# Expert rows transposed by their load, and one 32 by 32 product per head in the mamba stage

## The reference

```python
x = x + 0.5 * ffn(layernorm(x))      # mixture of experts
x = x + mamba(layernorm(x))
x = x + 0.5 * ffn(layernorm(x))      # the same weights again
```

## Time and profile before

| | us |
|---|---|
| median of 3 runs (1732.28 to 1732.94) | 1732.43 |
| the profiled execution | 1741.65 |
| its span | 1739.9 |
| TensorE busy | 1276.7 (73%) |
| VectorE busy | 1325.7 (76%) |
| ScalarE busy | 724.0 (42%) |
| GpSimd busy | 654.1 (38%) |
| DMA | 104.66 MB, mean 60 GB/s |

### The profile page before, as it was taken

The page is one execution under the profiler, slowest core; times in us unless marked ns, Lnnn a source line. Parts: engine busy times, 40 slices in busy tenths (PEclk is TensorE's granted clock), DMA queues, the critical chain, the costliest instruction groups (busy, mean ns, idle before and its releaser), DMA issues.

```text
span 1739.9 us, 32954 instructions
## 1 busy us (share of the span) xinstructions
PE 1276.7 (73%) x10560; PEld 961.0 (55%) x10560; DVE 1325.7 (76%) x3687; ACT 724.0 (42%) x1586; POOL 654.1 (38%) x832
## 2 busy tenths in 40 slices
PE   3426999947887787777888777688876551799990
PEld 3416999933545455454545445454544441799990
DVE  5964777758988888888888888898885664577776
ACT  2323555514444444444444444444444220355550
POOL 3873333323434343333424343333422376233330
PEclk9999999968878888888878788888878555899995
DMA  8543333310000000000000000000000022333328
GB/s 216 183 168 88 95 97 94 84 34 13 16 22 13 25 14 18 20 16 21 15 24 14 24 13 18 20 16 22 16 16 11 33 86 89 89 94 93 94 81 302
DMA packets 86838, 104.66 MB, mean 60 GB/s; under 512 B 18192, under 2 KB 66320, under 8 KB 86672
## 3 DMA queue, kind: packets, MB, share of 16 engines
q1 hardware_dynamic: 67856, 59.31, 13.2%
q0 software_dynamic: 14208, 39.05, 6.1%
q10 hardware_dynamic: 4608, 4.20, 0.7%
HBM read 50.88 MB, written 43.23 MB: 54 GB/s over the span
## 4 chain that ended last, share of the span: by engine, by line
PE 35%; DVE 22%; SPq 13%; POOL 9%; DMA 8%; issue 8%; ACT 5%; another core or an unknown queue 0%; POOLq 0%; DVEq 0%; ACTq 0%
SPq L1068 11%; PE bank L641 11%; PE bank L655 11%; DMA yg<-ychosen 5%; POOL disp L545 4%; ACT y L1115 4%; PE bank L1175 4%; DVE cv L876 3%; DVE cv L879 3%; PE bank L1242 2%; POOL arena L1028 2%; PE bank L1225 2%; DVE X L816 2%; PE bank L624 2%; DMA y<-y 1%
## 5 line engine op out<-in xcount | busy, mean ns | idle before, releaser
L590 POOL DMA_INDIRECT ychosen<-arena,didx x144 | 139.8, 971 | 295.1 <-ACT arena L687 280.1
L641 PE MATMUL bank<-arena,weights 128*128 128x128 f16 x3456 | 221.0, 221 | 0.0
L655 PE MATMUL bank<-weights,arena 128*128 x1728 | 211.5, 273 | 0.0
L641 PEld LDWEIGHTS bank<-arena,weights 128*128 x3456 | 203.3, 99 | 0.6 <-issue 0.3
L676 ACT ACTIVATE arena<-bank 128x512 f32<-128x512 f32 x144 | 86.0, 597 | 240.9 <-issue 140.3
L717 DVE TENSOR_TENSOR arena<-arena 128x512 f32<-128x512 f32 x144 | 99.8, 693 | 105.8 <-ACT arena L676 104.4
L1206 PE MATMUL bank<-arena,cst 128*128 128x512 f32 x256 | 172.4, 810 | 0.0
L655 PEld LDWEIGHTS bank<-weights,arena 128*128 128x128 f16 x1728 | 163.2, 98 | 16.4
L545 POOL DMA_INDIRECT disp<-arena,sloti x128 | 132.6, 1036 | 65.2 <-issue 39.8
L876 DVE TENSOR_SCALAR cv<-U,vec 128x128 f32<-128x128 f32 x160 | 141.7, 948 | 0.0
L1014 POOL TENSOR_TENSOR Hs<-Hs,dd 64x512 f32<-64x512 f32 x32 | 34.3, 1071 | 282.4 <-DVE yi L916 268.3
(11 more groups left out here) (168 smaller groups left out, 2646.7 us busy)
## 6 DMA issues: line engine op xcount, KB each, us to landing
arena<-disp SPq DMA_DIRECT2D x144, 129.5 KB
arena<-in_w SPq DMA_DIRECT2D x16, 512.0 KB
yg<-ychosen SPq DMA_DIRECT2D x32, 256.0 KB, 2.8
y<-y SPq DMA_DIRECT2D x512, 16.0 KB, 1.8
arena<-ychosen SPq DMA_DIRECT2D x32, 256.0 KB, 5.9
X<-in_x SPq DMA_DIRECT2D x32, 128.0 KB, 4.6
out<-X ACTq DMA_DIRECT2D x32, 128.0 KB, 6.1
ychosen<-arena,didx POOLq DMA_INDIRECT x144
```

Source lines behind the costliest of these rows:

```text
L590: pool.indirect_dma_start(ychosen, bass.IndirectOffsetOnAxis(ap=didx[:, t % NIDX:t % NIDX + 1], axis=0), ysb[t % YB][:, :], None).then_inc ...
L641: mm = pe.matmul(o, chunk(where, 2 * ("hl".index(w) * WN + c * HID + m * P), P), v, start=c == 0 and n_ == 0, stop=c == KD - 1 and n_ == 2)
L655: mm = pe.matmul(o, x, chunk(where, 2 * ((2 + "hl".index(w)) * WN + c * D), D), start=c == 0 and n_ == 0, stop=c == KH - 1 and n_ == 2)
```

## The change

The expert load becomes two: one that transposes the 512 halves into `xTh` (now eight buffers), and a small one for the last 6 halves of each row into `xtail`. TensorE's `turn` and VectorE's copy are gone; SP waits for `up` in place of `turned`. In mamba each pair's 64x64 product becomes two products, each with 32 weight columns and 32 moving columns, all into bank 6; ScalarE copies a half at once, and the two waits that bank 7 needed are gone.

```diff
-XIN, YB, HB = 4, 3, 3
+XIN, YB, HB = 8, 3, 3
...
-        xin = [carve(ROW, F16) for p in range(XIN)]
-        xTh = [carve(4 * P, F16) for p in range(2)]
+        xTh = [carve(4 * P, F16) for p in range(XIN)]
+        xtail = [carve(ROW - 2 * D, F16) for p in range(XIN)]
...
                 if t >= XIN:
-                    sp.wait_ge(S("turned"), n - XIN + 1)
+                    sp.wait_ge(S("up"), n - XIN + 1)
                     sp.wait_ge(S("didx"), n - XIN + 1)
-                sp.dma_start(xin[t % XIN][:, :], disp[ds(at, P), :]).then_inc(S(f"xin_{t % XIN}"), 16)
+                sp.dma_start(xTh[t % XIN].rearrange("p (c t) -> p c t", t=P), disp[ds(at, P), 0:2 * D], transpose=True)\
+                    .then_inc(S(f"xin_{t % XIN}"), 16)
+                sp.dma_start(xtail[t % XIN], disp[ds(at, P), 2 * D:ROW]).then_inc(S(f"xtail_{t % XIN}"), 16)
...
-            def turn(t):
+            def up(t):
                 n = r * NS + t
                 pe.wait_ge(S(f"xin_{t % XIN}"), 16 * (t // XIN + 1 + r * (NS // XIN)))
                 if n >= 2:
-                    pe.wait_ge(S("xth"), n - 1)
-                for c in range(4):
-                    m = pe.transpose(banks[t % 2].bitcast(F16)[:, c * P:(c + 1) * P], xin[t % XIN][:, c * P:(c + 1) * P],
-                                     ident16)
-                m.then_inc(S("turned"), 1)
-
-            def up(t):
-                n = r * NS + t
-                pe.wait_ge(S("xth"), n + 1)
-                if n >= 2:
                     pe.wait_ge(S("hr"), n - 1)
-                x = xTh[t % 2]
+                x = xTh[t % XIN]
...
-                dve.wait_ge(S("turned"), n + 1)
-                if n >= 2:
-                    dve.wait_ge(S("up"), n - 1)
-                dve.tensor_copy(xTh[t % 2][:, :], banks[t % 2].bitcast(F16)[:, 0:4 * P]).then_inc(S("xth"), 1)
+                dve.wait_ge(S(f"xtail_{t % XIN}"), 16 * (t // XIN + 1 + r * (NS // XIN)))
...
-                for n in range(2):
-                    for x in range(2):
-                        j = 2 * g + x
-                        o = y1[j * QT:(j + 1) * QT, :].rearrange("t (b r e) -> t r b e", b=B, e=HP)
-                        u = banks[6 + n][j * QT:(j + 1) * QT, :].rearrange("t (r x b e) -> t r x b e", x=2, b=B, e=HP)
-                        m = act.activation(o[:, n * 8:(n + 1) * 8], u[:, :, x], ACT.Copy)
-                m.then_inc(S("m_y1"), 1)
+                rows = slice(2 * g * QT, 2 * (g + 1) * QT)
+                act.activation(y1[rows, :].rearrange("t (b r e) -> t r b e", b=B, e=HP),
+                               banks[6][rows, :].rearrange("t (r b e) -> t r b e", b=B, e=HP), ACT.Copy).then_inc(S("m_y1"), 1)
...
             def inter(k, p):
                 pe.wait_ge(S("m_state"), k + 1)
-                after(pe, "m_y1", k * 2)
...
-                    pe.wait_ge(S("m_state"), k + 2)
...
-                mv_ = R[p].rearrange("p (g r c) -> p g r c", g=2, c=2 * QT)
+                mv_ = R[p].rearrange("p (g r x t) -> p g r x t", g=2, x=2, t=QT)
                 bv = bd.rearrange("p (g x r c) -> p g r x c", g=2, x=2, c=B * HP)
                 for r in range(NH // 4):
-                    n, c = r // 8, r % 8
-                    m = pe.matmul(banks[6 + n][2 * g * QT:2 * (g + 1) * QT, c * 64:(c + 1) * 64], mv_[:, g, r], bv[:, g, r],
-                                  start=True, stop=True)
+                    for x in range(2):
+                        j = 2 * g + x
+                        m = pe.matmul(banks[6][j * QT:(j + 1) * QT, r * B * HP:(r + 1) * B * HP], mv_[:, g, r, x], bv[:, g, r, x],
+                                      start=True, stop=True)
```

More of the change, by code:

```diff
@@ L661, in experts_pe @@
                     expert(t)
-                    turn(t)
                 if 1 <= t <= NS:
@@ L698, in take @@
                 n = r * NS + t
-                dve.wait_ge(S("turned"), n + 1)
-                if n >= 2:
-                    dve.wait_ge(S("up"), n - 1)
-                dve.tensor_copy(xTh[t % 2][:, :], banks[t % 2].bitcast(F16)[:, 0:4 * P]).then_inc(S("xth"), 1)
+                dve.wait_ge(S(f"xtail_{t % XIN}"), 16 * (t // XIN + 1 + r * (NS // XIN)))
                 if t >= NIDX:
                     dve.wait_ge(S(f"yst_{t % YB}"), 16 * ((t - NIDX) // YB + 1) + r * YST)
-                x = tail(xin[t % XIN])
+                x = xtail[t % XIN].bitcast(F32)
                 dve.tensor_scalar(place[t % 2][:, :], x[:, 2:3], tabf[:, t:t + 1], x[:, 0:1],
```

## The result

The changed kernel takes 1711.34 us (1710.53 to 1712.57, 4 runs) beside 1732.36 us for the kernel before: ratio 0.9879, 95% interval 0.9862 to 0.9896. It is 21 us faster; 44 us were forecast, that is 1688 us. On one of these the changed kernel itself came to 0.9862 (0.9842 to 0.9882).

What follows compares the result with a forecast made beforehand. TensorE was taken to bound the expert stages, and a chain of waits through ScalarE's copies, the moves and `yg` each mamba turn. Experts 31.7 plus mamba 12 made 44 us: 1732.4 to 1688 us, range 1679 to 1702.

Steps and rivals of the forecast that it cites:

- TensorE's 0.22 us a tile: Expert stages: without the transposes each tile's period falls from 2.87 to 2.65 us, 31.7 us over 144 tiles.
- The load's price on SP: Expert stages: SP's issuing of both loads comes to about 1.7 us a tile, within the 2.65 us period; no cost.
- The rival's own bound: Expert loads: transposing load becomes the bound, chance 0.22; SP alone could do it if that issue took over 1.2 us.
- small pieces on the DMA engines: Expert stages: one mechanism of the 0.22 rival; 16 pieces a row make 5.2 us a tile, 2055 us in all.
- The copies in mamba: Mamba: a half's copies are 0.93 us shorter, the second half's on the chain; about 12 us less in all.
- this cap: Mamba: GpSimd's work on Hs holds X, so 1.05 us of wait a turn remains; 12 us gained, not 27.
- The products: Mamba: the 64 records of the smaller products stay at about 2.1 us a half, covered by 1.9 us; cost zero.
- the lower bound of 27: Mamba: smaller products' records at least 27 ns apart, read from records of 8 columns; 1.7 us a half.
- "Zero" for the first load: Expert stage start: 1.5 us saved, twice, set against a later landing of the new first load; zero net.
- The third rival: Mamba: 32x32 products cost as much each as 64x64 ones, delaying `yg`; 1740 us, slower; chance 0.08.
- The second: Mamba: rival that GpSimd does not hold X when `yg` comes early; 27 us gained, 1673 us; chance 0.08.

Runs made afterwards that it cites:

- e3: Changed kernel with the small load and its own address reading moved from SP's queue to ScalarE's: 1693.81 us, ratio 0.9710 to the kernel before.
- e2: Only the expert edit, on the kernel before, mamba as it was: 1734.85 us beside 1744.31, ratio 0.9943.
- e4: Changed kernel with the small load issued twice on SP for each tile, the second into an unread buffer: 1794.64 us, ratio 1.0291 to the kernel before.
- e6: Only the mamba edit on the kernel before, but ScalarE still copies a half in four pieces, out of bank 6: 1739.10 us beside 1742.66, ratio 0.9975.
- e7: Changed kernel with GpSimd's product on Hs put off until VectorE has added the loaded rows to X: 1705.91 us, ratio 0.9781 to the kernel before.
- e1: Only the mamba edit, on the kernel before, expert part as before: 1725.35 us beside 1744.31, ratio 0.9894.
- e5: The changed kernel again with no edit, beside new runs of the kernel before: 1717.57 us beside 1742.66, ratio 0.9862.

## Why the prediction was wrong

**TensorE's 0.22 us a tile: right.** e3 shows the period that was forecast, 2.65 us, once nothing else stands ahead of it.

**The load's price on SP: the step that failed.** "SP comes to about 1.7 us and has 0.9 us left for a longer transposing issue." It was the right question, but no row gave the issue's price, and the sum of 44 us put it at nothing. Four terms make up SP's tile: 1.22 us transposing issue, 0.43 small issue, 0.28 + 0.16 address, and half a microsecond in short steps of 0.02 to 0.05 us; 2.62 to 2.65 us, and 2.78 with the pauses. The present load's instruction takes 0.3 us, the new one 0.9 us more. That uses the margin up. The common step of 2.62 us alone would still have left TensorE's 2.65 us as the bound; the pauses, which the prediction did not reckon with, come on top. (2.78 - 2.65) x 144 = 19 us of the 22 that are missing. What causes the pauses is open. The rival's own bound, "if the transposing issue took over 1.2 us", was met by 1.22 us; its main mechanism, small pieces on the DMA engines, was not: 690 packets of 17.5 ns are 0.76 us a tile on 16 engines, where the prediction had 640 of 36 ns. The size: 9.1 us by the profiles and 9.5 in e2 for 31.7 forecast. Taking one term, the small load's issue, off SP (e3) gives 26 us, doubling it (e4) costs 75.

What I had from the Trainium skill ("DMA: Bandwidth & Descriptors", "Latency and other measured facts", 261 GB/s for a transposing DMA) spoke of the transfer and was no help, since the issue bounds.

**The copies in mamba: right, mechanism and size.** The second half's copy (0.59 for 1.54 us) stands on the chain, e6 shows it. X is held by GpSimd, and ends 0.8 us after Hs, as forecast; e7 shows that this cap is real, for without it another 14 us come. For 28 turns the forecast was 11 us, and X's wait and work together fell by 10.8 us. The difference of e1 and e6, 14 us, agrees with the forecast's 12 within its uncertainty.

**The products: a term put at zero that was worth about 4 us.** This is the smaller miss: mamba gave 18.5 us (e1) for 12. 1.21 us for 64 records is 19 ns each, below the lower bound of 27. That bound was read from records at the lower level of TensorE's clock (granted 0.50 from 1442.5 to 1443.1 us), while the products of a half ran at the upper level in both kernels (granted 1.00 from 806.39 to 808.47 us before and from 823.7 to 824.9 us after). The second half's products don't hold up its copy (they end at 824.92, the copy starts at 830.00 us); that was right. But the sum asked only whether the products hold anything up and not what an earlier TensorE sets free. L887 took 952 ns on average before and 813 in e6, where X waits as before; in 32 turns that is 4.5 us, of which VectorE's step just ahead (L844) takes a part back: it took 0.60 us in the turn at 839 us, where L887 was short, and 0.23 us at 779 us, where it was long. The turns of e6 are 0.08 us shorter than before on average (28 turns), so part of its 4.4 us lies elsewhere or in the noise. That GpSimd's L1021 beside it is the cause I read from the timeline of single turns; no run takes it apart, nor the products from the two dropped waits.

**"Zero" for the first load** was near: from SP's first issue to the first `up` product are 143.2 to 146.4 us in place of 141.6 to 145.2, 0.4 us less.

The third rival (products too dear) didn't occur. The second (X not held, mamba 27 us) didn't either: e7 shows that X was held.

## What to carry to other kernels

A transposing DMA cost four times as much at its issue here as a plain one (1.22 us for 0.30), and the queue that issues it is an engine with a budget: add up all that it does for a tile (address, waits, each instruction, small loads as well as large ones) and leave a margin for pauses before counting on the work that the DMA takes off TensorE. If it comes out short, another engine's queue can take a part. Here the queue's usual step, 2.62 us for a bound of 2.65, left no room for the pauses. Where a wait is shortened, look at what else becomes free to collide there: putting GpSimd's product behind VectorE's sum gave as much again as the shorter copies.

## What the runs showed of the hardware that was not expected

- The issue of a transposing DMA held SP's queue for 1.2 us, whether for 512 or 256 columns of 128 rows (1224 and 1200 ns medians; single ones went down to 0.72 us in e5); a plain one with a register address took 0.3 to 0.43 us.
- Single-precision products with 32 weight columns and 32 moving columns, going by turns to two 32-partition groups of one bank, came 19 ns apart, 1.21 us for 64 records; with 64 by 64 they came 62 ns apart. The Trainium skill, "TensorE: Matmul & The Clock Gate", Part 3, says that products whose results lie in different 32-partition groups run side by side. The pace agrees, but no run puts them all into one group, so it is not shown that this is the reason. The Trainium skill, "TensorEngine Tiling (Array Packing)", "Instruction Overhead", gives about 60 cycles of overhead for each matmul. A product here is two records: 38 ns or 91 cycles of 2.4 GHz a product, 19 ns or 46 cycles a record, so the figure is not contradicted as one for a product. The page's warning against cutting a small dimension did not come true: the cut products took 1.21 us for 2.08.
- TensorE's granted clock fell in mamba from 0.82 to 0.77 on average, with more idle time ahead of L1250 (5.8 us on average for 3.0 before), whose four products took 1.12 us at a granted clock of 0.50 in place of 0.66 us at 1.00. Between 430 and 1300 us no wait of VectorE's is for these products, and the turns were shorter than before all the same.
